# The expert layer of a four-block program: padded tiles per expert, or unpadded tiles walked as a staircase

## The reference

```
probs = softmax(x @ gate_w.T)                      # 2048 x 64
topk_w, topk_idx = top_k(probs, 6); topk_w /= sum(topk_w)
combine = sum(one_hot(topk_idx, 64) * topk_w)
h = silu(einsum('th,eih->tei', x, experts_w1))     # 64 experts, 176 wide
y = einsum('tei,ehi->teh', h, experts_w2)
routed = einsum('teh,te->th', y, combine)
g, u = split(x @ shared_gate_up.T)                 # 352 wide each
out = layernorm(x + routed + (silu(g) * u) @ shared_down.T)
```

## Time and profile before

| | us |
|---|---|
| median of 3 runs | 1451.08 |
| the profiled execution | 1450.56 |
| its span, first to last instruction | 1448.8 |
| PE busy | 1165.2 |
| DVE busy | 827.0 |
| POOL busy | 550.8 |
| ACT busy | 520.3 |

### The profile page before, as it was taken

One profiled execution on the slowest core, in us unless ns is written; L12 is line 12 of the kernel. 1 busy time (PEld: TensorE's weight loads), 2 busy tenths in 40 slices (PEclk: granted clock), 3 DMA queues, 4 the chain that ended last, 5 costly groups with the idle time before them and its releaser, 6 DMA issues. The chain is left out here.

```text
span 1448.8 us, 19530 instructions
## 1 busy us (share of the span) xinstructions
PE 1165.2 (80%) x6223; PEld 677.3 (47%) x6223; DVE 827.0 (57%) x1604; ACT 520.3 (36%) x1052; POOL 550.8 (38%) x564
## 2 busy tenths in 40 slices
PE   5589999999999689989896418699999987878522
PEld 2242222222222245665464402389998876744311
DVE  6499999999997565436556489412221211114525
ACT  1137677777777422202351100133333332210000
POOL 6002447673636510012201006444444443235673
PEclk9799999999999989999997555599999998989755
DMA  4960631443100400000000100499999999842333
GB/s 133 184 151 8 91 40 26 54 57 39 26 12 14 152 3 0 1 1 1 0 1 0 60 0 0 126 297 310 315 316 302 300 273 226 235 137 69 102 102 91
DMA packets 142039, 154.26 MB, mean 106 GB/s; under 512 B 50641, under 2 KB 110898, under 8 KB 141874
## 3 DMA queue, kind: packets, MB, share of 16 engines
q1 hardware_dynamic: 106338, 98.19, 26.8%
q0 software_dynamic: 12288, 33.57, 9.2%
q10 hardware_dynamic: 23312, 21.24, 4.4%
HBM read 117.81 MB, written 32.51 MB: 104 GB/s over the span
## 5 line engine op out<-in xcount | busy, mean ns | idle before, releaser
L495 ACT ACTIVATE l_ret_store<-attn_st 128x512 f32<-128x512 f32 x512 | 280.0, 598 | 104.2 <-PE attn_st L406 94.4
L519 DVE TENSOR_REDUCE attn_neg<-attn_mx 128x8 f32<-128x1024 f32 x256 | 298.8, 1200 | 13.8 <-PE attn_mx L386 12.9
L1715 DVE COPY exp_y_sb<-exp_y_ps 128x256 f32<-128x256 f32 x160 | 67.9, 425 | 292.4 <-PE exp_y_ps L1660 273.6
L1626 POOL DMA_INDIRECT exp_rows<-x_rows,moe_tok_i x160 | 151.1, 944 | 191.1 <-PE exp_xt_ps L1640 172.2
L1651 PE MATMUL exp_h_ps<-exp_xt,exp_w 128*88 128x128 f32 x1280 | 173.2, 280 | 26.3 <-DMA exp_w<-in_w 25.3
L406 PE MATMUL attn_st<-attn_q_st,attn_k_st 128*128 128x512 bf16 x512 | 173.7, 383 | 5.0 <-DMA attn_q_st<-attn_neg_rows 2.7
L1660 PE MATMUL exp_y_ps<-exp_w,exp_ht 96*128 96x256 f32 x640 | 168.2, 386 | 1.3 <-ACT exp_ht L1687 1.3
L386 PE MATMUL attn_mx<-attn_k_st,attn_q_st 96*128 96x512 bf16 x512 | 154.9, 384 | 15.5 <-DVE attn_neg L519 15.2
L1651 PEld LDWEIGHTS exp_h_ps<-exp_xt,exp_w 128*88 128x88 f32 x1280 | 150.7, 160 | 34.2 <-DMA exp_w<-in_w 32.6
L418 PE MATMUL attn_o<-l_ret_store,l_ret_tab 128*32 128x512 f32 x1024 | 136.4, 605 | 0.8 <-ACT l_ret_store L495 0.8
L1680 ACT ACTIVATE exp_xt<-exp_xt_ps 128x256 f32<-128x256 f32 x160 | 61.4, 384 | 209.3 <-PE exp_xt_ps L1640 203.5
(11 more groups left out here) (235 smaller groups left out, 1616.4 us busy)
## 6 DMA issues: line engine op xcount, KB each, us to landing
exp_w<-in_w SPq DMA_DIRECT2D x320, 176.0 KB
y_rows<-exp_y_sb ACTq DMA_DIRECT2D x160, 128.0 KB
parts<-l0b_front SPq DMA_DIRECT2D x32, 192.0 KB
attn_k_st<-parts SPq DMA_DIRECT2D x48, 128.0 KB, 7.8
attn_q_st<-parts SPq DMA_DIRECT2D x48, 128.0 KB, 8.4
l_ret_tab<-in_tables SPq DMA_DIRECT2D x4, 1024.0 KB
exp_rows<-x_rows,moe_tok_i POOLq DMA_INDIRECT x160
keep_x_t<-in_x_t SPq DMA_DIRECT2D x4, 512.0 KB
```

What stands on the lines that cost most here:

```text
L495: act.activation(probs[s % 2][:, h], st_ps[n % BANKS][:], ACT.Exp, scale=SCALE0).then_inc(exp_done, 1)
L519: dve.tensor_reduce(neg[m % 2][:, i], mx_ps[slot["score", n] % 2][:].rearrange("p (j k) -> p j k", k=P), AX.X, ALU.max, negate=True).then_ ...
L1626: pool.indirect_dma_start(rows[b % RB][:], None, a["x_rows"], bass.IndirectOffsetOnAxis(ap=tok_i[:, b:b + 1], axis=0)).then_inc(rows_in[b ...
L1715: dve.tensor_copy(y_sb[b % YB][:], y_ps[b % 2][:, 0:E]).then_inc(y_in, 1)
```

## The change

Experts no longer get whole tiles. The 12,288 pairs, sorted by expert, are laid without padding into `FULL` = 96 tiles. A tile can hold rows of several experts, and an expert can reach over several tiles; walking down the tiles and experts together gives at most 96 + 63 = 159 steps (tile, expert). Each step multiplies the whole tile by that expert's weights; rows of other experts in it are computed and dropped.

- `route` finds the steps (`leaves`, `owner_f`), and instead of a token per slot a code per step and row: token tile, choice and lane in one number (`hot_high` is now indexed by tile plus expert). `dst_i` [128, 160] says where a step's row is written; rows that are not the expert's get an index beyond the buffer. A transposition and a matmul with `of_tile` fold the 160 step columns back into 96 tile columns for `tok_i`.
- `experts` gathers and transposes each of the 96 tiles once; ScalarE keeps it in a store in SBUF (`keep_tile`) and, for each of the 159 steps, reads the step's tile number into a register and copies that tile out of the store into one of three buffers (`take_tile`). The result is no longer written by ScalarE but scattered by GpSimd (indirect DMA with a bounds check) to the row of its token tile, choice and lane; out-of-bounds rows are skipped. Scatters lag behind the gathers by 2 to 20 steps. The result buffers are 24 instead of 8.
- `combine` loads the six results of a token tile with one dense DMA on SyncE's queue, eight tiles ahead; GpSimd's 96 gathers go. DVE's and TensorE's work is as before.

The diff, cut to its core:

```diff
@@ -1362,7 +1362,12 @@
 
-TILES = -(-(TOK * TOP // P + EXPERTS) // 8) * 8
+FULL = TOK * TOP // P
+STEPS = FULL + EXPERTS - 1
+TILES = STEPS + 1
+KPAD = 8
+NOWHERE = 1 << 20
+Y_ROWS = P + NT * KPAD * P
@@ -1447,11 +1461,13 @@
             ordered(pool.memset(before[:], 1.0))
-            ordered(pool.memset(upto[:], 1.0))
+            ordered(pool.memset(below[:], 1.0))
...
-            ordered(pool.affine_select(out=upto[:], in_=upto[:], compare_op=ALU.is_ge, fill=0.0,
-                                       base=0, pattern=[[1, P]], channel_multiplier=-1))
+            ordered(pool.affine_select(out=below[:, 0], in_=below[:, 0], compare_op=ALU.is_gt, fill=0.0,
+                                       base=0, pattern=[[1, EXPERTS]], channel_multiplier=-1))
+            ordered(pool.affine_select(out=below[:, 1], in_=below[:, 1], compare_op=ALU.is_ge, fill=0.0,
+                                       base=0, pattern=[[1, EXPERTS]], channel_multiplier=-1))
@@ -1479,12 +1495,10 @@
             pe.matmul(m_ps[0:EXPERTS, 0:1], sums[:, NT], ones[:, 0:1], start=True, stop=True).then_inc(counted, 1)
-            pe.wait_ge(vc, A_VC + 3)
-            pe.matmul(m_ps[:, 0:EXPERTS], n_tiles[:], before[0:EXPERTS, 0:EXPERTS], start=True, stop=True)
-            pe.matmul(m_ps[:, EXPERTS:2 * EXPERTS], n_tiles[:], upto[0:EXPERTS, 0:EXPERTS],
+            pe.wait_ge(vc, A_VC + 1)
+            pe.matmul(t_ps[:, 0:2 * EXPERTS], count[:], below[:].rearrange("p a e -> p (a e)"),
                       start=True, stop=True).then_inc(based, 1)
-            pe.wait_ge(vc, A_VC + 5)
@@ -1492,6 +1506,16 @@
+
+            pe.wait_ge(coded, 1)
+            for i in range(2):
+                mm = pe.transpose(t_ps[0:TILES // 2, i * P:(i + 1) * P],
+                                  code[:].rearrange("p (j i) -> p i j", i=2)[:, i], ident[:])
+            mm.then_inc(code_turned, 1)
+            pe.wait_ge(code_kept, 1)
+            for i in range(2):
+                mm = pe.matmul(t_ps[:, 2 * P:2 * P + FULL], code_t[:, i], of_tile[:, i], start=(i == 0), stop=(i == 1))
+            mm.then_inc(tiled, 1)
@@ -1542,18 +1566,22 @@
             dve.wait_ge(counted, 1)
-            chain(dve.tensor_scalar(count_i[:, 0:1], m_ps[0:EXPERTS, 0:1], float(P - 1), None, ALU.add))
-            chain(dve.tensor_single_scalar(count_i[:, 1:2], count_i[:, 0:1], 7, ALU.logical_shift_right))
-            chain(dve.tensor_copy(n_tiles[:], count_i[:, 1:2].to_broadcast([EXPERTS, P])))
+            chain(dve.tensor_copy(count[:], m_ps[0:EXPERTS, 0:1].to_broadcast([EXPERTS, P])))
             dve.wait_ge(based, 1)
-            chain(dve.tensor_scalar(base[:], m_ps[:, 0:EXPERTS], float(P), None, ALU.mult))
-            chain(dve.tensor_copy(ends[:], m_ps[:, EXPERTS:2 * EXPERTS]))
+            chain(dve.tensor_copy(base[:], t_ps[:, 0:EXPERTS]))
+            chain(dve.tensor_scalar(ends_i[:, 0], t_ps[:, EXPERTS:2 * EXPERTS], 1.0, -1.0, ALU.max, ALU.add))
+            chain(dve.tensor_single_scalar(ends_i[:, 1], ends_i[:, 0], 7, ALU.logical_shift_right))
+            chain(dve.tensor_tensor(leaves[:], ends_i[:, 1], iota[:, 0:EXPERTS], ALU.add))
             for i in range(2):
-                chain(dve.tensor_scalar(past[:, i], ends[:], tile_no[:, i:i + 1], None, ALU.is_le))
-            chain(dve.tensor_reduce(owner_f[:], past[:], AX.X, ALU.add))
-            chain(dve.tensor_scalar(owner_f[:], owner_f[:], float(EXPERTS - 1), None, ALU.min))
+                chain(dve.tensor_scalar(past[:, i], leaves[:, 0:EXPERTS - 1], tile_no[:, i:i + 1], None, ALU.is_lt))
+            chain(dve.tensor_reduce(owner_f[:, 0], past[:], AX.X, ALU.add))
+            chain(dve.tensor_tensor(owner_f[:, 1], tile_no[:], owner_f[:, 0], ALU.subtract))
+            chain(dve.tensor_scalar(owner_f[:, 1], owner_f[:, 1], float(FULL - 1), None, ALU.min))
             dve.tensor_copy(owner_i[:], owner_f[:]).then_inc(owned, 1)
+            for i in range(2):
+                chain(dve.tensor_scalar(of_tile[:, i], iota[0:TILES // 2, 0:FULL],
+                                        owner_f[0:TILES // 2, 1, i:i + 1], None, ALU.is_equal))
@@ -1566,32 +1594,46 @@
             chain(dve.tensor_copy(low[:], low_i[:]))
-            dve.tensor_copy(high[:], high_i[:]).then_inc(split, 1)
+            dve.tensor_tensor(high[:], high_i[:], best_f[:, :, 0:TOP], ALU.add).then_inc(split, 1)
...
-                dve.tensor_scalar(hot_high[:, n % HOTS, 0], iota[:], high[:, t, k:k + 1], float(t),
+                dve.tensor_scalar(hot_high[:, n % HOTS, 0], iota[:], high[:, t, k:k + 1], float(t * KPAD + k + 1),
...
-            chain(dve.tensor_scalar(tok_f[:], m_ps[:, 0:TILES], float(P), None, ALU.mult))
-            chain(dve.tensor_tensor(tok_f[:], m_ps[:, TILES:2 * TILES], tok_f[:], ALU.add))
-            chain(dve.tensor_copy(tok_i[:], tok_f[:]))
+            chain(dve.tensor_scalar(part[:], m_ps[:, 0:TILES], float(P), None, ALU.mult))
+            dve.tensor_tensor(code[:], m_ps[:, TILES:2 * TILES], part[:], ALU.add).then_inc(coded, 1)
+            dve.wait_ge(code_turned, 1)
+            dve.tensor_copy(code_t[:], t_ps[0:TILES // 2, 0:2 * P].rearrange("p (i r) -> p i r", i=2)
+                            ).then_inc(code_kept, 1)
+            chain(dve.tensor_scalar(none[:], part[:], 0.0, float(NOWHERE), ALU.is_equal, ALU.mult))
+            dve.wait_ge(coded, 1)
+            chain(dve.tensor_tensor(dst_f[:], code[:], none[:], ALU.add))
+            chain(dve.tensor_copy(dst_i[:], dst_f[:]))
+            dve.wait_ge(tiled, 1)
+            chain(dve.tensor_scalar(code_i[:], t_ps[:, 2 * P:2 * P + FULL], float(-P), None, ALU.add))
+            chain(dve.tensor_single_scalar(tok_hi[:], code_i[:], 10, ALU.logical_shift_right))
+            chain(dve.tensor_single_scalar(tok_hi[:], tok_hi[:], 7, ALU.logical_shift_left))
+            chain(dve.tensor_single_scalar(code_i[:], code_i[:], P - 1, ALU.bitwise_and))
+            chain(dve.tensor_tensor(tok_i[:], tok_hi[:], code_i[:], ALU.add))
...
-        tok_i, owner, ident = keep["tok_i"], keep["owner"], keep["ident"]
-        B, RB, YB = 6, 10, 8
+        tok_i, dst_i, owner, ident = (keep[n] for n in ("tok_i", "dst_i", "owner", "ident"))
+        B, RB, YB, XB, LEAD, LAG_END = 6, 12, 24, 3, 10, 18
...
-        xt = [sb(f"xt{i}", [P, KT, P]) for i in range(2)]
+        tiles = sb("tiles", [P, FULL, KT, P])
+        xt = [sb(f"xt{i}", [P, 1, KT, P]) for i in range(XB)]
@@ -1616,28 +1658,49 @@
             for n in range(B):
-                sp.wait_ge(w_in[n], 32 * len(range(n, TILES, B)))
+                sp.wait_ge(w_in[n], 32 * len(range(n, STEPS, B)))
...
-            for b in range(TILES):
-                if b >= RB:
-                    pool.wait_ge(turned, b - RB + 1)
-                pool.indirect_dma_start(rows[b % RB][:], None, a["x_rows"], bass.IndirectOffsetOnAxis(
-                    ap=tok_i[:, b:b + 1], axis=0)).then_inc(rows_in[b % RB], 16)
+            def gather(t):
+                if t >= RB:
+                    pool.wait_ge(turned, t - RB + 1)
+                pool.indirect_dma_start(rows[t % RB][:], None, a["x_rows"], bass.IndirectOffsetOnAxis(
+                    ap=tok_i[:, t:t + 1], axis=0)).then_inc(rows_in[t % RB], 16)
+            def scatter(b):
+                pool.wait_ge(y_in, b + 1)
+                pool.indirect_dma_start(a["y_rows"], bass.IndirectOffsetOnAxis(ap=dst_i[:, b:b + 1], axis=0),
+                                        y_sb[b % YB][:], None, bounds_check=Y_ROWS - 1, oob_is_err=False
+                                        ).then_inc(y_out[b % YB], 16)
+            for t in range(LEAD):
+                gather(t)
+            sent = 0
+            for b in range(STEPS):
+                if b + LEAD < FULL:
+                    gather(b + LEAD)
+                lag = 2 + LAG_END * min(b, FULL) // FULL if b < FULL else max(2, 2 + LAG_END - (b - FULL) // 2)
+                while sent <= b - lag:
+                    scatter(sent)
+                    sent += 1
+            for b in range(sent, STEPS):
+                scatter(b)
             for n in range(RB):
-                pool.wait_ge(rows_in[n], 16 * len(range(n, TILES, RB)))
+                pool.wait_ge(rows_in[n], 16 * len(range(n, FULL, RB)))
+            for n in range(YB):
+                pool.wait_ge(y_out[n], 16 * len(range(n, STEPS, YB)))
...
-            def turn(b):
-                pe.wait_ge(rows_in[b % RB], 16 * (b // RB + 1))
-                if b >= 2:
-                    pe.wait_ge(xt_in, b - 1)
+            def turn(t):
+                pe.wait_ge(rows_in[t % RB], 16 * (t // RB + 1))
+                if t >= 2:
+                    pe.wait_ge(tile_in, t - 1)
                 for k in range(KT):
-                    mm = pe.transpose(xt_ps[b % 2][:, k * P:(k + 1) * P], rows[b % RB][:, k * P:(k + 1) * P], ident[:])
+                    mm = pe.transpose(xt_ps[t % 2][:, k * P:(k + 1) * P], rows[t % RB][:, k * P:(k + 1) * P], ident[:])
@@ -1648,7 +1711,7 @@
```

(76 more changed lines are left out.)

47 lines of the change are left out of this document (28 added, 19 removed).

## The result

The changed kernel took 1480.99 us (median of 4 runs, 1476.52 to 1483.41) against 1451.99 for the kernel before beside it: ratio 1.0177, 95% interval 1.0142 to 1.0211. It is slower by 1.8%; forecast were 1397 us and a range of 1362 to 1448. On another chip, further down, the same kernel is faster than the kernel before by 2.8%, at 1399 us. So there are two questions: what makes it slow here, and what of the forecast holds where that is absent.

A forecast was written before the change was run, and what follows sets the result against it. TensorE at 1.96 us a step bounded the expert stage, DMA just under it; after the change GpSimd would be the bound. Profiled 1450.6 + 5 routing - 33 expert stage - 26 combine stage = 1397 us, range 1362 to 1448.

The forecast's parts named there:

- the expert stage's path: Expert stage: GpSimd's 255 DMAs at 1.25 us, then the last TensorE steps, give 333 us against 366.4, -33.
- late signals: Combine stage: 35 us in which DVE sat although the TensorE work it needed had ended by the records.
- Rival A: Combine stage: signals stay late, tied to TensorE starved at half clock, not to gathers; all 35 us remain, 1420 us; chance 0.18.
- Rivals B and C: Expert stage: B (0.12), scatters at 1.53 us, 1434 us; C (0.13), scatters above 1.68 us, slower, 1508 at 2.0.
- Rival D: Expert stage: the port lock reaches DVE's PSUM copies, each 0.42 us copy holds a DMA; +59, 1456 us; chance 0.03.
- Rival E: Expert stage: ScalarE's dynamic copy sits behind TensorE, the turns' saving is lost; +14, 1411 us; within the forecast's 0.52.
- forecast +5: Routing: extra small DVE operations and the fold through TensorE add 5 us, bounds 3 and 9.
- forecast 208: Expert stage: the last gather is the 164th DMA, issued at 18.9 + 151 x 1.25 = 208 us.
- six buffers: Expert stage: six weight buffers hide SyncE's 1.81 us a step against TensorE's 1.74 over the 66 last steps, 4.6 us.
- the full -38: Combine stage: dense loads replace gathers and all late signals go, 119 us instead of 157.2; the lower bound.
- The 12 us of late signals: Combine stage: a third of the 35 us assumed to stay, making the forecast -26 instead of -38.

The follow-up runs named there:

- e11_again: The changed kernel unaltered, run on chip 9, where no signal came late: 1399.10 us against 1439.06 for the kernel before, ratio 0.972.
- e10_tiny: Kernel before plus a 16-column gather on GpSimd, into buffers nobody reads, in every other expert-stage step: 1494.81 us, ratio 1.030 on chip 0.
- e4_narrow: Changed kernel with scattered rows cut from 256 to 16 columns, combine adding rows of x instead: 1395.03 us, ratio 0.972 on chip 12.
- The hybrid: Changed kernel without scatters: dense result writes by ScalarE, combine gathers on GpSimd as before. Chip 12: 1409.09 us; chip 9 (e12_hybrid): 1409.35; chip 0: 1433.74.
- e5_pause: Changed kernel with a 128x256 memset on GpSimd behind each of its 255 DMAs: 1437.20 us, ratio 1.000 on chip 12.

## Why the prediction was wrong

**The step that failed** is the expert stage's path, "242 DMAs are left, 302 us: GpSimd ends at +321". It lets GpSimd issue back to back for 300 us at no price to the others. I had seen in the combine stage that late signals "fell in stretches of back-to-back gathers, which vanish", and I costed only their going. The change builds such a stretch into the longest stage. What the runs put in its place: on a chip that has the lateness, 255 DMAs in a row hold up signals of TensorE for several us at a time. The stage is 432.6 us in the first measurement, 430.8 and 430.1 on chips 8 and 0, and 352.3 on chip 9, so 78 to 80 us of lateness for a term that I had set at nothing. Part of the 80 is TensorE's granted clock: 0.89 over 940 to 1220 us, for 0.99 in e11_again. e10_tiny shows that more DMAs on GpSimd suffice, without a scatter or the new chain on ScalarE; e4_narrow, that the scattered bytes cost next to nothing on a chip without lateness (350.8 for 352.3; where signals are late it wasn't tried).

**Rival A had the cause reversed.** It tied the signals to a starved TensorE and not to GpSimd's DMAs. The changed kernel's own combine stage tests that on the late chip: TensorE is as starved as A asks, at a granted clock of 0.74 (0.69 before), but GpSimd has no DMAs, and no wait in the stage is remote. In the line the third number from the end is the clock:

```profile
1362.00:1477.00 115.00, 80.77 (x192) 43.07 (x192) 71.48 (x175) 7.14 (x12) 4.77 (x4) 0.74 0.42 128
```

In e10_tiny, the other way round, a TensorE that had been full gets late signals from more DMAs on GpSimd.

**Rivals B and C asked for a dear scatter.** There was none: 159 at a mean of 996 ns, and gaps of 0.30 where GpSimd waits for nobody, so 1.30 us of pitch (bound 1.53, C's threshold 1.68). C gave the sign that came, by another cause; the time it named, 1508, was off too.

**Rival D** is refuted by the same row and by e11_again, where 16 or 17 DMAs go in 20 us with DVE's PSUM copies between them. By the Trainium skill (SBUF — State Buffer, section "SBUF: two separate sides") fp32 SBUF-to-SBUF copies in the two-port mode shut descriptor writing out. The copies here read PSUM, which the page doesn't name, and and GpSimd's DMAs beside 159 of them are 0.97 and 1.00 us long on average, the longest scatter 1.02, not longer by the copies' 0.42; a copy of the kind that the page names isn't in this stage.

**Rival E** did not happen: e11_again's TensorE is busy 20.00, 19.95 and 19.23 of 20 us from 940 to 1000 with the dynamic copy in its chain, and its last steps, which have no turn, do go at 1.74 us where their weights are there.

**Where signals are prompt the mechanism was right, and two sizes off.** In e11_again, whose span is 50.9 us below that of the kernel before: routing +5.1 (forecast +5). GpSimd's last gather starts 210.6 us after its first (forecast 208). The four starts of its timeline that count, the last two at the stage's end:

```profile
927.23 1.24 POOL L1668 DMA_INDIRECT exp_rows<-x_rows,moe_tok_i  x1 [13.45 <-POOLq L58]
...
1137.86 0.98 POOL L1668 DMA_INDIRECT exp_rows<-x_rows,moe_tok_i  x1 [0.30 <-issue]
...
1265.88 0.98 POOL L1673 DMA_INDIRECT y_rows<-exp_y_sb,moe_dst_i  x1 [0.30 <-issue]
1279.47 0.41 SPq L1804 DMA_DIRECT2D comb_w_up<-in_w_sh_up  x1
```

The stage is 352.3 us, not 333. The last result is copied at +337.5, where the forecast had 326: the last 66 steps go at 1.82 (11 in 20 us), not 1.74, which is 5 of the 11. A step alone has the forecast pitch (results copied at 1190.99, 1192.73 and 1194.47), but TensorE stops for weights:

```profile
1190.99 0.42 DVE L1776 COPY exp_y_sb<-exp_y_ps 128x256 f32<-128x256 f32 x1 [1.46 <-PE exp_y_ps L1723]
1192.73 0.42 DVE L1776 COPY exp_y_sb<-exp_y_ps 128x256 f32<-128x256 f32 x1 [1.32 <-PE exp_y_ps L1723]
```
```profile
PEld exp_h_ps L1714 <- DMA exp_w<-in_w: 9.3, 17, 1.9
```

The second fence is the sum of such waits of TensorE's weight loads from 1140 to 1260 us, 9.3 us in 17. SyncE issues a step's weights every 1.8 us at best, as the prediction had read (1.81), and waits for a free buffer for only 0.9 us of this stretch. That six buffers would hide the difference over these steps is the part that failed.

Behind that comes a cost that I had not seen. GpSimd's last DMA ends 12.6 us before the next stage begins, and the DMA engines are idle for nearly all of them (the last but one number is their share):

```profile
1268.00:1278.00 10.00, 0.00 (x0) 0.00 (x0) 0.00 (x0) 0.00 (x0) 0.00 (x0) 0.50 0.00 0
```

I had allowed 3.7 (landing 2.5, end 1.2). The changed kernel has the same 12.6 (1349.12 to 1361.73). In the kernel before GpSimd's last gather ends 34 us ahead of the barrier, so that its drain there, of 4.6 us, lies under the last steps.

**The combine stage** is 116.0 us on the late chip and 114.4 on chip 9, not 131: the full -38 and some more. The 12 us of late signals that I kept were none, on either chip: with no DMA on GpSimd in this stage no signal was late. Its tile pitch is 3.80, forecast 3.79:

```profile
1393.96 3.42 DVE L1882 SCALAR_TENSOR_TENSOR keep_x<-comb_got,moe_weight,keep_x 128x256 f32<-128x256 f32 x6
1397.42 0.42 DVE L612 TENSOR_TENSOR keep_x<-comb_y,keep_x 128x256 f32<-128x256 f32 x1
1397.76 3.42 DVE L1882 SCALAR_TENSOR_TENSOR keep_x<-comb_got,moe_weight,keep_x 128x256 f32<-128x256 f32 x6
```

The 35 us that I had called late signals were mostly something else. The hybrid's combine stage gathers as the kernel before does; up to the last scaling it takes 146.7 and 145.0 us on chips 9 and 12, without a remote wait, and 155.0 on chip 0 (157.2 in the kernel before). So lateness was worth some 8 to 12 us of it. Where signals are prompt, DVE waits for gathers to land instead, 38.9 us in e12_hybrid where it had been 14.5:

```profile
DVE keep_x L1871 <- DMA comb_got<-y_rows,moe_out_i: 38.9, 53, 1.9
```

The rest of the gain, 32 us on chip 9, comes from the gathers' going itself.

So 1399 on chip 9 beside the forecast 1397 is in part luck: the expert stage was forecast 19 us too short and the combine stage 17 too long. And against the kernel before on its own chip the gain is 40 us, not 54, for that kernel takes 12 us less there (1439.1 for 1451.1) and the changed one 2 more than forecast. That this is its own signals being prompt is inferred, from the hybrid's combine stage.

**What stays open.** Why chips differ (0 and 8 have it, 9 and 12 don't), what in GpSimd's issue holds the signals, and why a pause of 0.3 us shortens hold-ups but doesn't prevent them. No run separates GpSimd's descriptor writing from its semaphore traffic, and the kernel before has no profile here on a chip of the second kind.

## What to carry to other kernels

A stall that coincides with some pattern of issue, and whose cause the trace doesn't give, has to be priced for every place where a change creates that pattern, not only where the change removes it. Software DMAs on GpSimd belong in real gaps: 10 or 11 in 20 us cost the other engines nothing that showed in the traces, while in this change's nearly unbroken row they made a stage of 352 us 78 to 80 us longer on two of the chips met. And a verdict of 2% either way should be reached on more than one chip, with the kernel before beside it: here the sign changed with it.

## What the hardware showed beyond that

- The same kernel's time depends on the chip: the kernel before takes 1436 and 1439 us on chips 12 and 9, and 1449 to 1452 on chips 0 and 8.
- A gap of 12.6 us between the last of a long row of GpSimd DMAs and the end of the barrier behind it, the same with full and paused issue (12.3 us in e5_pause), on quiet chips and late ones. The trace's instruction records have GpSimd in a drain for 9.1 of them. The kernel before has one of 9.2 us too, from 1438.8 to 1448.0 us, of which 2.7 lie under the last scalings; without gathers in that stage it takes 1.4 us (e11_again), which can account for the 3.3 us saved behind them.
- Idle pauses can pay, but are no cure: a memset of 331 ns behind each GpSimd DMA gained 8 us on a late chip, where 30 us of lateness stayed, and cost some 35 on a quiet one.
